# Attention kernel of a macaron layer: scores of two groups behind every second gate, one bank for both FFNs' sums, and other places for the projections and for the probabilities' low part

## The chip, the cores and the metric

The kernel runs on one core of one Trainium2 chip. The metric is the device time of the whole program in microseconds (us); less is better.

## The reference

One layer of the "macaron" form on x of 8 x 512 tokens with D = 512. LN is a layer norm without gains.

```
x = x + 0.5 * FFN(LN(x))        # FFN "A"
x = x + ATTN(LN(x))
x = x + 0.5 * FFN(LN(x))        # FFN "C", the same weights
FFN(x):  gu = x @ ternary(w_gate_up).T ; gate, up = split(gu)      # 2048 wide each
         h = silu(gate) * up ; return rms_norm(h) @ ternary(w_proj).T
ATTN(x): q, k, v = x @ Wq.T, x @ Wk.T, x @ Wv.T                     # 32 heads of 16
         scores = q @ k.T / 4, masked to a window of the 128 keys before each query
         return (softmax(scores) @ v) @ Wo.T
```

A query sees its own block of 128 tokens and the block ahead of it. In the first block of each sequence of 512 tokens there is only its own. The weights of the FFN are quantised to three values by groups of 64; the kernel does that on the chip too.

## The kernel before, in words

The 4096 tokens are 32 blocks of 128 rows (`NB` = 32). An instruction stream is written by hand for each engine, and semaphores order them; no scheduler moves anything. After the weights are prepared (the first 150 us or so), every engine runs the same loop `for step in range(FIRST_STEP, STEPS)` with a `step_of(step)` of its own. A block enters every 8 steps, and the stages of a block stand at fixed offsets: stage X of block b is at step 8b + X. What one step of an engine does, and in what order, is the order of the lines in its `step_of`. Below, r is the step modulo 8; **r = 1, 3, 5, 7 are called odd steps**.

- *FFN.* The hidden 2048 columns are 4 quarters of 512 (`NC` = 4). In the steady state A has its quarters at r = 0 to 3, C at r = 4 to 7, so each step has one quarter. TensorE (PE) multiplies its gate half (`up(.., 0, ps_g)`, 8 matmuls of 512 columns) and its up half (`up(.., 1, ps_u)`, 8 more), and two steps later the down product of it (`down`, 8 more, into `ps_y`). ScalarE (ACT) takes tanh of the gate, VectorE (DVE) multiplies (`gated`, L859; `hidden`, L865), ACT and DVE split the result in a high and a low f16 half (`hh`, L605 and L850), and a DMA transpose makes `ht` of it. `spread` gives the quarters of a few blocks at either end of the program other steps, so that there are steps without a quarter.
- *Attention.* The heads are 8 groups of 4. Group g of block b has its step at 8b + `SCORES` + g, one in every step. PE multiplies the scores (`scores`: 4 matmuls with only 48 rows of the array each, of 256 columns, the two halves of the array in turn), DVE adds the mask and takes the row maxima (`masked_max`, L876: 4 instructions, each with a read of its maximum), ACT takes bias and exps (L726, L731) and the high f16 half of the probabilities (L743), DVE the low half (L850, prob), two DMA transposes make `pt`, and PE multiplies by v (`prob_v`, 16 matmuls of 33 columns). After each second group DVE normalises (`normalise_o`, L886 to L891).
- *Projections.* Q, K, V and the output projection are 12 matmuls of 512 columns each (`project`) into one bank, `ps_m`. Q, K, V and the output projection stand at r = 0, 1, 3 and 7, at the end of PE's step.
- *PSUM.* There are eight banks: `ps_s` (two, scores), `ps_g`, `ps_u`, `ps_y` (two: one for A's sums and one for C's), `ps_o` and `ps_m`.

The order within a step of the steady state on PE is: gate, down (of two steps ago), up, scores of the next step's group, probabilities times v, a projection. PE waits in this order for `d_gate` and `d_h` (DVE has emptied `ps_g`, `ps_u`), `t_h` (ht has landed), `d_mx` (DVE has read the scores of the group before) and `t_ph`, `t_pl` (pt has landed).

On DVE a step is: `normalise_o`, `masked_max` of one group, the low part of q, k or v, `gated`, the low part of the last step's probabilities, `add_output`, `hidden`, the low part of the attention output (`oh`), `add_ffn`, the statistics of a layer norm (`norm_stats`, L841 to L845), the low part of `hh`. All DMAs of the loop are issued by SyncE (SP), in its order.

Of the kernel before, what the change touches and what calls it, by code (L numbers as in the profile page):

```python
# [15 lines left out]
P = 128  # L16
# [8 lines left out]
def macaron(nc, x, Wq, Wk, Wv, Wo, w_gate_up, w_proj, out):  # L25
# [55 lines left out]
    with ExitStack() as ctx:  # L81
# [174 lines left out]
        t_q, t_k, t_o = sem("t_q"), sem("t_k"), sem("t_o")  # L256
# [41 lines left out]
        assert len(AT_STEP) == len(GATES) == 2 * NB * NC - NC  # L298

# [99 lines left out]
        def _(sp):  # L399
# [55 lines left out]
            for step in range(FIRST_STEP, STEPS + 1):  # L455
# [7 lines left out]
                if b is not None:  # L463
                    sp.wait_ge(a_k, b + 1)
                    sp.wait_ge(d_k, b + 1)
                    need(sp, p_s, 16 * (b - 2))
                    transpose(kt[:, :, b % BPS, :], k4[:, :, :, :].rearrange("p a b c -> p (a b c)"), t_k)
                b, g = group_at(step, PROB)
                if b is not None:
                    need(sp, p_pv, 8 * b + g - 1)  # L470
                    sp.wait_ge(a_ph, 8 * b + g + 1)
                    first = first_half(b)
                    transpose(pt[:, g % 2, 0, first:2, :, :].rearrange("p a b c -> p (a b) c"),
                              prob[:, g % 2, 0, first:2, :, :].rearrange("p a b c -> p (a b c)"), t_ph[g % 2])
                    sp.wait_ge(d_pl, 8 * b + g + 1)
                    transpose(pt[:, g % 2, 1, first:2, :, :].rearrange("p a b c -> p (a b) c"),
                              prob[:, g % 2, 1, first:2, :, :].rearrange("p a b c -> p (a b c)"), t_pl[g % 2])
# [11 lines left out]
                if b is not None and in_steps("A", b):  # L489
                    normalised_t("A", b, p_up["A"], 8 * b)  # L490
                b = block_at(step, SPLIT_O)
# [7 lines left out]
                b = complete("C", step, 3)  # L499
# [3 lines left out]
                b = block_at(step, LN_A - 8)  # L503
# [98 lines left out]
        def _(act):  # L602
# [69 lines left out]
            def step_of(step):  # L672
# [13 lines left out]
                if b is not None:  # L686
                    need(act, t_k, 16 * b)
# [21 lines left out]
                if block_at(step, SPLIT_O) == LAST:  # L709
                    output_hi(LAST)  # L710
# [6 lines left out]

                b = block_at(step, SPLIT_O)
                if b is not None and b < LAST:
                    output_hi(b)  # L720
# [14 lines left out]
                s, bf, c = ffn_at(step)  # L735
                if s:
                    hidden_hi(s, bf, c, place(step), 4 * bf + c + 1 + (NC if s == "A" else 0))

                b, g = group_at(step, SCORES)
                if b is not None:  # L740
                    act.wait_ge(a_exp, 8 * b + g + 1)
                    need(act, t_ph[g % 2], 16 * (4 * b + g // 2))
                    act.activation(prob_part(prob[:, g % 2, 0, :, :, :], b), prob_f32(b, g), ACT.Copy).then_inc(a_ph, 1)  # L743

# [4 lines left out]
        def _(dve):  # L749
# [118 lines left out]
            def masked_max(b, g):  # L868
# [3 lines left out]
                for o in range(2):  # L872
                    dve.wait_ge(p_s, 16 * b + 2 * g + o + 1)
                    for pair in range(2):
                        hd = 4 * g + 2 * pair + o
                        m = dve.tensor_tensor_reduce(masked[:, g % 2, 2 * pair + o, first:2 * P],  # L876
                                                     ps_s[:, o * CH + pair * 2 * P + first:o * CH + (pair + 1) * 2 * P],
# [17 lines left out]
            def add_ffn(s, b, done):  # L895
                dve.wait_ge(p_dn[s], 4 * b + 4)
                dve.wait_ge(g_rms[s], b + 1)
                dve.scalar_tensor_tensor(out=slot(b), in0=ps_y[s][:, :], scalar=rms_inv[s][:, 0:1], in1=slot(b),  # L898
# [47 lines left out]
            def step_of(step):  # L946
                b, g = group_at(step, NORM)
                if b is not None and g % 2:
                    normalise_o(b, g // 2)

                b, g = group_at(step, SCORES)
                if b is not None:
                    masked_max(b, g)
# [31 lines left out]
                if block_at(step, SPLIT_O) == LAST:  # L985
                    output_lo(LAST)
# [292 lines left out]
```

## Time and profile before

| | |
|---|---|
| median of 3 runs | 2029.98 us (2029.53 to 2031.16) |
| the profiled execution | 2030.56 us, span of its profile 2028.7 us |
| PE busy | 1919.7 us, 95% |
| DVE busy | 1541.2 us, 76% |
| ACT busy | 1493.1 us, 74% |
| DMA queue q1 | 75.9% of 16 engines' span |
| granted clock of PE, mean | 0.98 |

The span is that of the profiled execution, from the first to the last instruction; 1.9 us of that execution's time lie around it. A group's busy time counts each matmul until its modelled end, which overlaps the start of the next, so groups of PE add up to more than the span. How far PE is from its peak is better read from the starts of successive groups in the timeline. Full speed is 2.4 GHz, and the lower level is half of it.

### The profile page before, as it was taken

The page shows a single profiled execution, that of the slowest core. Times are in us where ns is not written, and L with a number is a line of the kernel's source. Part 1 is how long each engine was busy: PE and PEld are TensorE (multiplying, and loading weights), DVE is VectorE, ACT ScalarE, POOL GpSimd, SP SyncE. Part 2 cuts the span into 40 slices and gives each one's busy share as a digit, 9 for nine tenths or more (in the row PEclk, how much of TensorE's full clock was granted, in tenths as well). Part 3 has the DMA queues.
Part 4 walks back from the last instruction along what each step waited for, and adds up shares of the span by engine and source line. Part 5 has one row for each costly group of instructions (what it writes and reads, how often), then busy time and mean ns, then how long its engine had stood idle before and what let it go on. Part 6 is the DMA issues. An engine that isn't in the chain of part 4 may idle for free. (4 is left out here: it accounts for less than half of the span.)

```text
span 2028.7 us, 37471 instructions
## 1 busy us (share of the span) xinstructions
PE 1919.7 (95%) x12447; PEld 898.9 (44%) x12688; DVE 1541.2 (76%) x4079; ACT 1493.1 (74%) x2871; POOL 510.9 (25%) x559
## 2 busy tenths in 40 slices
PE   6678899999999999999999999999999999999887
PEld 3353344444444444444444444444444444444332
DVE  8966788777876888777777888777786788777673
ACT  6837777777776777777776777777776777768672
POOL 2012222232223222322222223222223232221100
PEclk8889999999999999999999999999999999999898
DMA  7336888788887878777896788878886788768772
GB/s 233 121 71 112 147 153 147 132 141 159 149 156 126 156 145 153 136 145 150 154 159 125 138 155 153 149 131 154 159 155 120 141 153 165 144 120 154 131 136 52
DMA packets 1031648, 287.81 MB, mean 142 GB/s; under 512 B 1016096, under 2 KB 1017120, under 8 KB 1030944
## 3 DMA queue, kind: packets, MB, share of 16 engines
q1 hardware_dynamic: 1031456, 285.41, 75.9%
q8 instruction: 101, 1.65, 0.3%
q14 instruction: 91, 0.75, 0.1%
HBM read 25.17 MB, written 8.39 MB: 17 GB/s over the span
## 5 line engine op out<-in xcount | busy, mean ns | idle before, releaser
L731 ACT ACTIVATE masked<-masked,exp_bias,exp_scale 128x256 f32<-128x256 f32 (+1 forms) x1024 | 503.8, 562 | 8.6
L1095 PE MATMUL ps_yy<-wp_t,ht 128*128 128x512 bf16 x1978 | 481.0, 383 | 14.4 <-DMA ht<-hh 11.7
L1049 PE MATMUL ps_gu<-wgu_t,xt_A 128*128 128x512 bf16 x1940 | 473.8, 382 | 11.2 <-DVE hid L859 2.5
L1049 PE MATMUL ps_gu<-wgu_t,xt_C 128*128 128x512 bf16 x1958 | 472.6, 379 | 5.3 <-DMA xt_C<-xh 0.5
L605 ACT ACTIVATE hh<-hid 128x512 f16<-128x512 f32 x256 | 161.0, 629 | 276.3 <-DVE hid L865 271.0
L876 DVE CUSTOM_DVE_ANT_0 masked<-ps_s,mask 128x256 f32<-128x256 f32 (+1 forms) x1024 | 337.4, 385 | 0.7 <-PE ps_s L1085 0.6
L865 DVE SCALAR_TENSOR_TENSOR hid<-ps_gu,h_scale_u,hid 128x512 f32<-128x512 f32 x252 | 188.9, 750 | 185.0 <-PE ps_gu L1049 184.7
L1095 PEld LDWEIGHTS ps_yy<-wp_t,ht 128*128 128x128 f16 x2016 | 197.9, 99 | 254.5 <-DMA ht<-hh 13.5
L1049 PEld LDWEIGHTS ps_gu<-wgu_t,xt_A 128*128 128x128 f16 x2048 | 198.6, 98 | 243.3 <-issue 6.3
L1049 PEld LDWEIGHTS ps_gu<-wgu_t,xt_C 128*128 128x128 f16 x2048 | 193.4, 98 | 222.5 <-issue 2.4
L850 DVE TENSOR_TENSOR prob<-masked,prob 128x1024 f16<-128x1024 f32 (+1 forms) x256 | 278.9, 1089 | 2.4 <-ACT prob L743 2.4
L859 DVE SCALAR_TENSOR_TENSOR hid<-hid,ps_gu 128x512 f32<-128x512 f32 x256 | 175.8, 687 | 109.3 <-ACT hid L609 108.7
L544 POOL TENSOR_TENSOR xh<-xhat,xh 128x512 f16<-128x512 f32 x94 | 110.2, 1173 | 550.9 <-ACT xh L605 550.9
L850 DVE TENSOR_TENSOR hh<-hid,hh 128x512 f16<-128x512 f32 x256 | 176.2, 689 | 94.1 <-ACT hh L605 91.4
L743 ACT ACTIVATE prob<-masked 128x1024 f16<-128x1024 f32 (+1 forms) x256 | 239.2, 934 | 0.5
L609 ACT ACTIVATE hid<-ps_gu 128x512 f32<-128x512 f32 x256 | 150.1, 586 | 108.1 <-PE ps_gu L1049 104.4
L666 ACT ACTIVATE squares<-hid 128x512 bf16<-128x512 f32 x256 | 156.9, 613 | 0.0
L1107 PE MATMUL ps_om<-v,pt 128*128 128x33 f16 x3584 | 132.2, 178 | 5.8 <-DMA pt<-prob 5.8
L1107 PEld LDWEIGHTS ps_om<-v,pt 128*128 128x128 f16 x3584 | 106.7, 96 | 54.4 <-issue 47.2
L726 ACT ACTIVATE exp_bias<-row_max,prob_bias,neg_exp_scale 128x4 f32<-128x4 f32 x256 | 97.9, 382 | 30.1 <-DVE row_max L876 26.7
L1085 PE MATMUL ps_s<-kt,qt 48*128 48x256 f16 (+1 forms) x1024 | 93.7, 261 | 14.8 <-DVE row_max L876 14.8
L535 POOL TENSOR_TENSOR rstd_B<-var_eps_B,neg_half 128x1 f32<-128x1 f32 x32 | 28.5, 892 | 280.6 <-DVE var_eps_B L845 280.6
(148 smaller groups left out, 1892.8 us busy)
## 6 DMA issues: line engine op xcount, KB each, us to landing
stream<-in_L_attn_x_dram SPq DMA_DIRECT2D x32, 256.0 KB, 3.3
pt<-prob SPq DMA_TRANSPOSE x512, 3.2
out_dram<-stream SPq DMA_DIRECT2D x32, 256.0 KB, 2.4
prob<-in_L_ffn_w_gate_up_dram SPq DMA_DIRECT2D x4, 1024.0 KB, 5.6
ht<-hh SPq DMA_TRANSPOSE x256, 3.3
stream<-in_L_ffn_w_gate_up_dram SPq DMA_DIRECT2D x3, 1024.0 KB, 5.6
stream<-in_L_ffn_w_proj_dram SPq DMA_DIRECT2D x2, 1024.0 KB, 4.9
prob<-in_L_ffn_w_proj_dram SPq DMA_DIRECT2D x2, 1024.0 KB, 4.8
```

The lines of the kernel that those rows point to most:

```text
L605: act.activation(dst, src, ACT.Copy, scale=scale).then_inc(done, 1)
L609: act.activation(hid[:, n % 2, :], ps_g[:, :], ACT.Tanh, scale=0.5 * 2.0 ** -XS_LOG2).then_inc(a_tanh[s], 1)
L666: act.activation(squares[:, n % 2, :], hid[:, n % 2, :], ACT.Square, accum_out=sq_quarter[s][:, c:c + 1]).then_inc(a_sq[s], 1)
L731: t = act.activation(p, p, ACT.Exp, bias=exp_bias[:, 4 * g + h:4 * g + h + 1], scale=exp_scale[:, 0:1])
L743: act.activation(prob_part(prob[:, g % 2, 0, :, :, :], b), prob_f32(b, g), ACT.Copy).then_inc(a_ph, 1)
L850: dve.tensor_tensor(out=dst, in0=src, in1=hi, op=ALU.subtract).then_inc(done, 1)
L859: dve.scalar_tensor_tensor(out=hid[:, n % 2, :], in0=hid[:, n % 2, :], scalar=1.0, in1=ps_g[:, :], op0=ALU.add, op1=ALU.mult).then_inc(d_g ...
L865: dve.scalar_tensor_tensor(out=dst, in0=ps_u[:, :], scalar=scale, in1=hid[:, n % 2, :], op0=ALU.mult, op1=ALU.mult).then_inc(d_h[s], 1)
L876: m = dve.tensor_tensor_reduce(masked[:, g % 2, 2 * pair + o, first:2 * P], ps_s[:, o * CH + pair * 2 * P + first:o * CH + (pair + 1) * 2 ...
L1049: t = pe.matmul(bank[:, :], xt[s][:, part, k, :], wgu_t[:, k, at:at + CH], start=(k == 0 and part == 0), stop=(k == KD - 1 and part == 1))
L1095: t = pe.matmul(ps_y[s][:, :], ht[:, n % HRING, i, :], wp_t[:, 4 * c + i % 4, :], start=(c == 0 and i == 0), stop=(c == NC - 1 and i == 2 ...
L1107: t = pe.matmul(ps_o[:, at:at + VW], pt[:, g % 2, part, half, 2 * pair + o, :], v[:, at_block - 1 + half, hd, 0:VW], start=(n == 0), stop= ...
```

## The change

- The two sums `ps_y` of A and C become one bank. The bank freed is `ps_x`. A new table `ps_sc` gives even groups' scores the two banks of `ps_s`, and odd groups' scores the banks `ps_x` and `ps_m`; `ps_m` is the bank of the projections too.
- PE multiplies the scores of groups g and g+1 together, in every second step (g even, so r = 4, 6, 0, 2), behind the gate of the same step. The products with v stand between down and up. `scores` waits that the projection of two steps ago has been taken from `ps_m`, and each projection waits until DVE has read the scores of both groups (`d_mx`). The first down product of an FFN waits until the sum of the FFN before has been taken.
- The projections stand at r = 0 (Q), 2 (K), 4 (V) and 6 (output; the last block's stays where it was).
- DVE does `masked_max` of both groups in the even step, and the low part of the probabilities in the step of their exps, behind `hidden`. `normalise_o` and `add_ffn` stand ahead of `hidden`. The normalisation is one step earlier, and so are the split of the attention output (`SPLIT_O`) and C's layer norm.
- ACT makes the probabilities' high part ahead of the hidden split, not behind it.
- SP transposes the probabilities in the step of their exps. The transpose of k is two DMAs, of 4 and of 12 tiles, each with a semaphore of its own.

```diff
-    Q_AT, K_AT, V_AT = 8, 9, 11
+    Q_AT, K_AT, V_AT = 8, 10, 12
     SCORES = 12
-    PROB = SCORES + 1
     PV = SCORES + 2
-    NORM = PV + 1
-    SPLIT_O, WO_AT = NORM + 7, 23
-    LN_C, XHAT_C, SPLIT_C = 24, 25, 26
+    NORM = PV
+    SPLIT_O, WO_AT = NORM + 7, 22
+    LN_C, XHAT_C, SPLIT_C = 23, 24, 26
...
-    LAST_WO = 8 * LAST + WO_AT
+    LAST_WO = 8 * LAST + WO_AT + 1
...
-        ps_y = {"A": ps_yy[:, 0:CH], "C": ps_yy[:, CH:2 * CH]}
+        ps_y, ps_x = ps_yy[:, 0:CH], ps_yy[:, CH:2 * CH]
...
+        ps_sc = ((ps_s[:, 0:CH], ps_s[:, CH:2 * CH]), (ps_x, ps_m))
...
@@ vector, step_of @@
+                b, g = group_at(step, SCORES)
+                if b is not None and g % 2 == 0:
+                    masked_max(b, g)
+                    masked_max(b, g + 1)
...
+                b, g = group_at(step, SCORES)
+                if b is not None:
+                    prob_lo(b, g)
...
@@ tensor @@
+            def projections_taken(step):
+
+                for offset, done in ((Q_AT, d_q), (K_AT, d_k), (V_AT, d_v), (WO_AT, d_x2)):
+                    b = block_at(step, offset)
+                    if b is not None:
+                        pe.wait_ge(done, b + 1)
...
+                b, g = group_at(step, SCORES)
+                if b is not None and g % 2 == 0:
...
+                    need(pe, d_mx, 2 * (8 * b + g))
+                    projections_taken(step - 2)
...
+                    scores(b, g, ps_sc[0])
+                    scores(b, g + 1, ps_sc[1])
...
                 s, b, c = ffn_at(step - 2)
                 if s:
                     if c == 0:
-                        need(pe, d_x1 if s == "A" else d_x3, b)
+                        _, s0, b0, _ = QUARTERS[place(step - 2) - 1]
+                        pe.wait_ge(d_x1 if s0 == "A" else d_x3, b0 + 1)
                     down(s, b, c, place(step - 2))
...
                     pe.wait_ge(t_x["B"], 16 * (b + 1))
                     need(pe, d_x2, b - 1)
                     need(pe, d_v, b)
+                    need(pe, d_mx, 2 * groups_by(step + 1, SCORES))
```

The same wait on `d_mx` stands ahead of K, V and the output projection.

Two steps of PE (r = 5, 6) of a block in the steady state, before. L1049 is a gate or an up half, L1095 down, L1085 scores, L1107 probabilities times v, L1074 a projection:

```order
L1049 MATMUL ps_gu<-wgu_t,xt_C 128x512 x8
L1095 MATMUL ps_yy<-wp_t,ht 128x512 x8
L1049 MATMUL ps_gu<-wgu_t,xt_C 128x512 x8
L1085 MATMUL ps_s<-kt,qt 128x256 x4
L1107 MATMUL ps_om<-v,pt 128x33 x16
L1049 MATMUL ps_gu<-wgu_t,xt_C 128x512 x8
L1095 MATMUL ps_yy<-wp_t,ht 128x512 x8
L1049 MATMUL ps_gu<-wgu_t,xt_C 128x512 x8
L1085 MATMUL ps_s<-kt,qt 128x256 x4
L1107 MATMUL ps_om<-v,pt 128x33 x16
```

The same place in the change, from the down product of r = 5 to the output projection of r = 6 (an up half and a gate stand together in the third row):

```order
L1099 MATMUL ps_yy<-wp_t,ht 128x512 x8
L1111 MATMUL ps_om<-v,pt 128x33 x16
L1054 MATMUL ps_gu<-wgu_t,xt_C 128x512 x16
L1089 MATMUL ps_s<-kt,qt 128x256 x4
L1089 MATMUL ps_yy<-kt,qt 128x256
L1089 MATMUL ps_om<-kt,qt 128x256
L1089 MATMUL ps_yy<-kt,qt 128x256
L1089 MATMUL ps_om<-kt,qt 128x256
L1099 MATMUL ps_yy<-wp_t,ht 128x512 x8
L1111 MATMUL ps_om<-v,pt 128x33 x16
L1054 MATMUL ps_gu<-wgu_t,xt_C 128x512 x8
L1079 MATMUL ps_om<-wo,ot 128x512 x12
```

The eight score matmuls stand together in the even step, four of them into `ps_s` and four into `ps_yy` and `ps_om`, and the projection in `ps_om` follows 40 matmuls later in the same step.

DVE at the end of an odd step (r = 5) and the start of the next, in the change. L870 is `hidden`, L855 the low parts, L881 `masked_max`:

```order
L891 TENSOR_REDUCE o_sum<-ps_om 128x128
L892 RECIPROCAL row_inv<-ps_om 128x8
L896 TENSOR_TENSOR o_norm<-o_sum,row_inv 128x128
L903 SCALAR_TENSOR_TENSOR stream<-ps_yy,rms_inv_A,stream 128x512
L870 SCALAR_TENSOR_TENSOR hid<-ps_gu,h_scale_u,hid 128x512
L855 TENSOR_TENSOR prob<-masked,prob 128x1024
L855 TENSOR_TENSOR oh<-o_norm,oh 128x512
L846 BN_STATS st_B<-stream 128x6
L848 BN_AGGR mean_var_B<-st_B 128x2
L850 TENSOR_SCALAR var_eps_B<-mean_var_B 128x1
L855 TENSOR_TENSOR hh<-hid,hh 128x512
L881 ISA masked,row_max<-ps_s,mask 128x256
```

Before, the low part of `oh` and the statistics of B stood in different steps, and `prob` stood ahead of `hidden`; here all of them stand between `hidden` and the first of eight L881.

## Rows read from the trace of the kernel before

**Rows 1.** Busy time by stretch: us, busy (x count) of PE, PEld, DVE, ACT, POOL; PEclk; DMA share
```profile
186.90:246.30 59.40, 49.56 (x337) 22.08 (x340) 44.74 (x132) 45.44 (x87) 17.01 (x15) 0.94 0.84 140
400.00:800.00 400.00, 397.25 (x2616) 183.29 (x2667) 313.21 (x855) 306.86 (x603) 109.14 (x117) 1.00 0.83 148
1866.20:1962.30 96.10, 78.50 (x567) 34.84 (x577) 72.12 (x209) 72.39 (x134) 15.45 (x18) 0.89 0.73 134
```

**Rows 2.** Timeline of PE, steady state, one step and the next one's start: start, us, group
```profile
1025.43 1.89 PE L1049 MATMUL ps_gu<-wgu_t,xt_A 128*128 128x512 bf16 x8
1027.16 1.89 PE L1095 MATMUL ps_yy<-wp_t,ht 128*128 128x512 bf16 x7
1028.88 1.89 PE L1049 MATMUL ps_gu<-wgu_t,xt_A 128*128 128x512 bf16 x8
1030.71 0.39 PE L1085 MATMUL ps_s<-kt,qt 48*128 48x256 f16 x4
1031.03 0.57 PE L1107 MATMUL ps_om<-v,pt 128*128 128x33 f16 x16
1031.45 2.75 PE L1074 MATMUL ps_om<-wq,xt_B 128*128 128x512 f16 x12
1034.03 1.89 PE L1049 MATMUL ps_gu<-wgu_t,xt_A 128*128 128x512 bf16 x7
```

**Rows 3.** Timeline of DVE in the same steps: start, us, instruction [idle before <-releaser]
```profile
1028.59 1.22 DVE L850 TENSOR_TENSOR prob<-masked,prob 128x1024 f16<-128x1024 f32 x1
1029.73 0.74 DVE L982 SCALAR_TENSOR_TENSOR stream<-ps_om,out_scale,stream 128x512 f32<-128x512 f32 x1
1030.91 0.75 DVE L865 SCALAR_TENSOR_TENSOR hid<-ps_gu,h_scale_u,hid 128x512 f32<-128x512 f32 x1 [0.44 <-PE ps_gu L1049]
1031.58 0.69 DVE L841 BATCH_NORM_STATS2 st_C<-stream 128x6 f32<-128x512 f32 x1
...
1032.59 0.68 DVE L850 TENSOR_TENSOR hh<-hid,hh 128x512 f16<-128x512 f32 x1
1033.18 0.42 DVE L876 CUSTOM_DVE_ANT_0 masked<-ps_s,mask 128x256 f32<-128x256 f32 x1
...
1034.56 0.08 DVE L876 DVE_READ_ACCUMULATOR2_ANT row_max<- 128x1 f32 x1
...
1041.64 0.42 DVE L886 TENSOR_REDUCE o_sum<-ps_om 128x128 f32<-128x256 f32 x1
...
1042.47 0.42 DVE L876 CUSTOM_DVE_ANT_0 masked<-ps_s,mask 128x256 f32<-128x256 f32 x1
```

**Rows 4.** Timeline of ACT in the same steps
```profile
1027.36 0.60 ACT L609 ACTIVATE hid<-ps_gu 128x512 f32<-128x512 f32 x1 [1.24 <-PE ps_gu L1049]
...
1028.26 2.08 ACT L731 ACTIVATE masked<-masked,exp_bias,exp_scale 128x256 f32<-128x256 f32 x4
...
1032.91 1.04 ACT L743 ACTIVATE prob<-masked 128x1024 f16<-128x1024 f32 x1
```

**Rows 5.** The page's groups: splits of 512 columns on ACT (count, busy us, mean ns)
```profile
L605 ACT ACTIVATE hh<-hid 128x512 f16<-128x512 f32 x256 | 161.0, 629 | 276.3 <-DVE hid L865 271.0
```

**Rows 6.** DMA issues of the page: count, KB, us from issue to landing
```profile
pt<-prob SPq DMA_TRANSPOSE x512, 3.2
...
ot<-oh SPq DMA_TRANSPOSE x32, 3.3
```

**Rows 7.** Groups by form: the masks of the blocks that begin a sequence
```profile
L876 DVE CUSTOM_DVE_ANT_0 masked<-ps_s,mask 128x128 f32<-128x128 f32 x256 | 58.7, 285 | 0.6 <-PE ps_s L1085 0.6
```

**Rows 8.** Timeline of PE near the end of the program
```profile
1955.79 0.39 PE L1085 MATMUL ps_s<-kt,qt 48*128 48x256 f16 x4 [1.64 <-DVE row_max L876]
...
1956.80 3.19 PE L1095 MATMUL ps_yy<-wp_t,ht 128*128 128x512 bf16 x8
1961.37 0.55 PE L1107 MATMUL ps_om<-v,pt 128*128 128x33 f16 x16 [1.38 <-DMA pt<-prob]
...
1963.98 1.89 PE L1095 MATMUL ps_yy<-wp_t,ht 128*128 128x512 bf16 x8
...
1980.25 4.45 PE L1074 MATMUL ps_om<-wo,ot 128*128 128x512 f16 x12 [3.22 <-DMA ot<-oh]
```

More of the change, by code:

```diff
@@ L298, in macaron @@
         assert len(AT_STEP) == len(GATES) == 2 * NB * NC - NC
+        assert all(QUARTERS[n][1:3] == QUARTERS[n - n % NC][1:3] for n in range(len(QUARTERS)))
         def gate_at(step):
@@ L453, in _ @@
                 load_x(b)
-            for step in range(FIRST_STEP, STEPS + 1):
+            for step in range(FIRST_STEP, STEPS + 2):
                 b = block_at(step, Q_AT + 1)
@@ L466, in _ @@
                     need(sp, p_s, 16 * (b - 2))
[L467 to L477, printed above, removed]
+                    for part, pairs in enumerate((slice(0, 4), slice(4, HEADS // 2))):
+                        transpose(kt[:, pairs, b % BPS, :],
+                                  k4[:, 2 * pairs.start:2 * pairs.stop, :, :].rearrange("p a b c -> p (a b c)"),
+                                  t_k[part])
                 b = block_at(step, SPLIT_B)
@@ L498, in _ @@
                     hidden_t(s, b, c, place(step))
-                b = complete("C", step, 3)
+                b = complete("C", step, 4)
                 if b is not None:
@@ L946, in step_of, with add_output, prob_lo @@
             def step_of(step):
[L947 to L953, printed above, removed]
+                def add_output(b):
+                    dve.wait_ge(p_wo, b + 1)
+                    dve.scalar_tensor_tensor(out=slot(b), in0=ps_m[:, :], scalar=out_scale[:, 0:1], in1=slot(b),
+                                             op0=ALU.mult, op1=ALU.add).then_inc(d_x2, 1)
+                def prob_lo(b, g):
+                    need(dve, t_pl[g % 2], 16 * (4 * b + g // 2))
+                    take_lo(prob_part(prob[:, g % 2, 1, :, :, :], b), prob_f32(b, g),
+                            prob_part(prob[:, g % 2, 0, :, :, :], b), a_ph, 8 * b + g + 1, d_pl)
                 b = block_at(step, Q_AT + 1)
@@ L993, in step_of @@
                         attention_weight(n)
-                b = block_at(step, WO_AT + 1)
-                if b is not None and b < LAST:
-                    add_output(b)
+                b = complete("A", step, 2)
+                if b is not None:
+                    add_ffn("A", b, d_x1)
+                b = complete("C", step, 2)
+                if b is not None:
+                    add_ffn("C", b, d_x3)
                 s, bf, c = ffn_at(step)
@@ L1069, in attention_weight, with project, scores @@
                 t.then_inc(a_tr, 1)
-            def project(m, tokens, done):
+            def project(m, tokens, done, bank):
                 for k in range(KD):
                     for n, (part, w) in enumerate(((0, wat_hi), (0, wat_lo), (1, wat_hi))):
-                        t = pe.matmul(ps_m[:, :], tokens[:, part, k, :], w[m][:, k, :], start=(k == 0 and n == 0),
+                        t = pe.matmul(bank[:, :], tokens[:, part, k, :], w[m][:, k, :], start=(k == 0 and n == 0),
                                       stop=(k == KD - 1 and n == 2))
                 t.then_inc(done, 1)
-            def scores(b, g):
+            def scores(b, g, banks):
                 at_block = b % BPS
@@ L1246, in step_of @@
                     pe.wait_ge(d_q, b + 1)
-                    project(K, xt["B"], p_k)
+                    need(pe, d_mx, 2 * groups_by(step + 1, SCORES))
+                    project(K, xt["B"], p_k, ps_m)
                 b = block_at(step, V_AT)
```

121 lines of the change are left out of this document (59 added, 62 removed).

## The prediction

> **What bounds the kernel now.** First the busy time by stretch [rows 1]. In the steady state PE is busy for 397.25 of 400 us at full clock, while DVE is busy for 78% of the time and ACT for 77%. Only there does PE's own work set the time; it lasts from step 28 (about 246 us) to step 252 (about 1866 us), 112 pairs of steps. In the ramp (186.9 to 246.3 us) PE is busy for 83%, and near the end (1866.2 to 1962.3 us, steps 252 to 267) for 82% at a mean clock of 0.89. There DVE and ACT hold PE up, each 75% busy itself.
>
> A busy PE isn't a PE at its peak, so the timeline of PE comes next [rows 2]. Read the starts. The gate takes 1.73 us (1025.43 to 1027.16), down 1.72, up with what follows it 1.83, scores 0.32, the products with v 0.42, a projection 2.58. Gate, down and up have eight matmuls of one size each, so 0.10 of up's 1.83 us is a pause ahead of the scores. A step is 6.02 us, and a pair of steps with its one projection 14.62.
>
> Then DVE and ACT in the same steps [rows 3, 4], for how long after PE they can start and how long a thing keeps its engine (again from start to start): `hidden` starts 0.30 us after up is done (1030.61) and keeps DVE for 0.67; a low part of the probabilities 1.14; statistics 1.01 (1031.58 to 1032.59); a low part of 512 columns 0.59; normalising 0.83; four masks 1.38, with 0.08 for the last read. The tanh starts 0.20 after the gate is done, the exps 0.90 after the tanh's start, and exps and high part take 2.08 and 1.04.
>
> **What the change takes from PE.** Of two groups of scores, one pause of 0.10 goes. The second four matmuls stand behind four of their own kind. Eight full-size matmuls take 1.72 us, so 256 columns take 0.108. The two halves of the array have separate matmuls; if they run side by side, four cost 0.21 and not 0.32, as the other 0.11 is the change back to the whole array. I take this, since 0.32 is less than the 0.43 that four cost one after the other. The gain is 0.21 a pair; its bounds are 0.10 (the pause alone) and 0.30. A pair becomes 14.41: even step 1.73 + 0.10 + 0.32 + 0.21 + 1.72 + 0.42 + 1.73 + 2.58 = 8.81, odd step 1.73 + 1.72 + 0.42 + 1.73 = 5.60. Over 112 pairs that is **-23.5 us** (-11 to -34). The Trainium skill ("TensorEngine Tiling (Array Packing)", "Key Properties") says that changing the tiling mode drains the array, which is what the 0.10 looks like; by that rule the pause goes with every change of mode, whatever stands around it, and the term stays as it is.
>
> **What it adds: projections wait for masks.** An odd group's scores lie in `ps_m`, so the projection that ends the even step waits for eight masks, which DVE starts only when its odd step is over. Let T be the time at which PE ends the odd step. PE reaches the projection at T + 8.81 - 2.58 = T + 6.23.
>
> - r = 7 to 0, ahead of Q. ACT: tanh at T - 5.60 + 1.73 + 0.20, exps 0.90 later, high part done at T + 0.4, in time. DVE: `hidden` T + 0.30 to 0.97, low part of the probabilities to 2.11, statistics of C to 3.12, low part of `hh` to 3.71, then eight masks, 2.76 + 0.08: T + 6.55. With 0.05 for the semaphore (an estimate) PE starts at 6.60: **0.37 us late**.
> - r = 5 to 6, ahead of the output projection. `normalise_o` can start 0.3 us after the products with v, at T - 5.60 + 3.87 + 0.30 = T - 1.43, and is done at T - 0.55. Now ACT splits the attention output first (0.63 [rows 5]) and makes the high part of the probabilities after it: done at T + 1.15. DVE: low part of the probabilities 1.19 to 2.33, of `oh` to 2.93, statistics of B to 3.94, `hh` to 4.53, masks to 7.37; PE at 7.42: **1.19 us late**. The transpose of `oh`, issued at about T + 3.7 behind two of the probabilities, lands 3.3 us later [rows 6], at about 7.0. It is the next to be late, and covers half of what an earlier mask would give.
> - r = 1 to 2 and 3 to 4, ahead of K and V: no statistics in the odd step. `hh` ends at T + 2.70, the masks at 5.54, and PE comes 0.64 after them. No wait.
> - Blocks that begin a sequence (every fourth) have masks of 128 columns, 285 ns each where the others have about 420 [rows 7, 3], and half of the probabilities. 8 x 0.135 + 0.5 is more than 1.19: no wait.
>
> The other new waits cost nothing in the steady state. The one bank of sums is free when `add_ffn` is done, at about T + 0.1 (behind `normalise_o`), and down comes at T + 2.36. The projection is taken from `ps_m` by T - 2.9, and the scores come at T + 1.83. The first 4 tiles of kt are issued at about T - 2.3 and needed at T + 1.83; the other 12 only two steps later. The k transpose as two DMAs is one more of 31 a block. SP waits for the low part at r = 5 with `oh` and `hh` queued behind it, and `hh` isn't needed before T + 10.5.
>
> 21 of the blocks in the steady state aren't the first of a sequence: 21 x (0.37 + 1.19) = **+32.8 us**. Each of these waits rests on a chain of ten durations and I allow 0.2 on either: 24 to 41 us.
>
> **The ends.** In steps 252 to 267 many steps have no quarter, so PE reaches the projection sooner and waits for the masks longer. Laid out by hand from the same durations, the pairs from 252 on take 12.0, 15.8, 15.0, 10.3, 12.0, 16.5, 10.8 and 8.6 us, 101 in all, against the 96.1 of before [rows 1]. In three of them PE stands for 4 to 5 us and its projection runs at half clock, as 1980.25 shows (4.45 us for twelve matmuls instead of 2.75 [rows 8]). At the last output projection the 3.22 us wait for `ot` should go, since the products with v and the normalisation come earlier, and with it the 1.7 us of half clock. Together **+3 us**, and the bounds are -8 and +12, since a hand layout of unsteady steps can be off by half a microsecond in each. The ramp has four such pairs (steps 20 to 27): **+1.5 us** (-3 to +5).
>
> **Sum.** -23.5 + 32.8 + 3 + 1.5 = +13.8 on the profiled execution's 2030.56 gives 2044.4. The median of the runs is 0.6 lower: **2044 us**, 0.7% slower.
>
> **The rivals.**
>
> *Faster: masks come in time* (24%). If the masks end about 0.4 us sooner, Q no longer waits, the output projection waits for 0.8 at most, and the balance tips. The point is 0.9 us of waiting a block (21 x 0.9 = 19 us). For it: in the two pairs the sum hangs on some tenths of a chain of ten, and near the end PE is held up by `row_max` of the very group before [rows 8], a wait that pairs do away with. Against it: DVE has no idle time left in my chain for r = 5 and 7. With 0.4 us a block: -23.5 + 8 = -15 and nothing from the ends, 2015 us; with 0.8, 2023.
>
> *No change* (13%): waits of 1.0 to 1.3 a block and the ends even, 2026 to 2034.
>
> *The clock falls* (8%, one of the slower cases). A pause of 1.64 us near the end is followed by matmuls at half speed (3.19 us for eight instead of 1.89), one of 1.38 isn't [rows 8]. My wait for the output projection is 1.2 us, of which some 1.0 would show as idle. Should it tip the clock to 1.2 GHz, each costs 1.7 more: 21 x 1.7 = 36, 2080 us. The Trainium skill ("TensorE: Matmul & The Clock Gate", "HAM oscillation") describes a kernel whose every tile starts cold after a pause for data; by that rule it would be 2080. No row here shows it for pauses as short as mine.
>
> *The scores don't get cheaper* in pairs is in the range: 0.10 a pair instead of 0.21 adds 12 us, 2056.
>
> **Chances.** About 0.2% (4 us) can be told from no change. Forecast and its slower neighbours 55%, clock 8%: slower 0.63; faster 0.24; same 0.13. The range: 2044 with its own bounds (waits +-8, scores -10 to +12, ends -14 to +12, not all at once) is 2028 to 2062. Toward the faster rival it goes down to 2020, which leaves out about half of that; the clock's case is left out above.
>
> **What would show it.** In the changed kernel's PE waits, the projections wq and wo should wait for `row_max` about 0.2 to 0.4 and 1.0 to 1.2 us, 21 times each, and wk and wv not. The scores' first start in an even step should be 1.83 after the gate's, down 0.53 after that. The steady state should have blocks of 57.6 us where no mask waits and 59.2 us elsewhere, against 58.5. Wrong would be: no wait at wo (the faster rival), wait on `ot` instead, projections of 4.4 us in the middle of the program (the clock), or down starting 0.64 us after the scores.

## The result, and the profile after

| | before | after |
|---|---|---|
| median of 4 runs | 2029.76 us (2027.77 to 2031.16) | 2074.77 us (2073.75 to 2121.51) |
| ratio, 95% interval | | 1.0221 (1.0201 to 1.0241) |
| profiled execution, span | 2030.56, 2028.7 us | 2074.78, 2072.9 us |
| up to the gate of step 28 | 246.3 us | 255.1 us |
| steps 28 to 252 | 1620.1 us | 1645.0 us |
| step 252 to the start of the last output projection | 113.9 us | 125.9 us |
| from there to the end | 48.45 us | 46.85 us |

The change is slower by 2.2%, where 0.7% was forecast; the time lies outside the range. The highest run of after was a disturbed one and counts in no ratio. The sign was right, the size wrong in all three stretches: of the 44.2 us, the steady part takes 24.9 (forecast 9.3), the start 8.8 (1.5), and all that follows step 252 takes 10.5 (3).

The busy time of after, the page's first line and three stretches (columns as in [rows 1]: PE, PEld, DVE, ACT, POOL, then PE's clock):

```profile
PE 1919.5 (93%) x12688; PEld 913.7 (44%) x12688; DVE 1548.3 (75%) x4079; ACT 1507.5 (73%) x2871; POOL 481.0 (23%) x559
```

```profile
186.90:255.10 68.20, 54.47 (x366) 24.66 (x365) 47.49 (x142) 48.62 (x93) 16.93 (x15) 0.90 0.71 130
400.00:800.00 400.00, 389.64 (x2611) 183.47 (x2609) 306.67 (x840) 304.18 (x594) 100.29 (x116) 1.00 0.81 145
1900.10:2008.30 108.20, 81.79 (x594) 37.73 (x593) 72.86 (x209) 72.86 (x136) 16.03 (x18) 0.87 0.69 124
```

PE has as much to do as before (1919.5 us of busy time against 1919.7); DVE and ACT show 7 and 14 us more, and both are idle for a quarter of the span. PE's busy time in 400 us of the steady part fell from 397.25 to 389.64 [rows 1], at full clock: it waits.

**What PE gained.** The timeline of PE in after, the end of an odd step and the even step with the output projection:

```profile
1033.25 3.61 PE L1054 MATMUL ps_gu<-wgu_t,xt_C 128*128 128x512 bf16 x16
1036.80 0.39 PE L1089 MATMUL ps_s<-kt,qt 48*128 48x256 f16 x4
1037.03 0.27 PE L1089 MATMUL ps_yy<-kt,qt 48*128 48x256 f16 x1
...
1037.34 1.90 PE L1099 MATMUL ps_yy<-wp_t,ht 128*128 128x512 bf16 x8
1039.08 0.56 PE L1111 MATMUL ps_om<-v,pt 128*128 128x33 f16 x16
1039.48 1.89 PE L1054 MATMUL ps_gu<-wgu_t,xt_C 128*128 128x512 bf16 x8
1042.47 2.75 PE L1079 MATMUL ps_om<-wo,ot 128*128 128x512 f16 x12 [1.10 <-DVE row_max L881]
1045.06 1.89 PE L1054 MATMUL ps_gu<-wgu_t,xt_C 128*128 128x512 bf16 x8
```

Down starts 0.54 us after the scores; 0.53 was forecast. The second group costs 0.21 us, and the gain of 0.21 a pair is there. (Between the scores and the projection stand 8, 16 and 8 matmuls, 32 and not the 40 that the section on the change gives.) Read the last wait against the starts: up starts at 1039.48 and takes 1.73, so PE could have gone on at 1041.21, and it started at 1042.47. It lost 1.26 us and the row shows 1.10. Each shown wait of such a kind is 0.16 us too small, because the end of the matmul before it is modelled.

**What it lost in the steady part.** PE's waits in after from 270 to 1870 us (columns: us in all, times, longest):

```profile
PE ps_om L1079 <- DVE row_max L881: 21.4, 34, 1.1
PE ps_om L1079 <- DMA ot<-oh: 19.0, 14, 1.9
PE ps_s L1089 <- DMA kt<-k: 0.5, 1, 0.5
```

That is 40.9 us shown in 49 waits, and with 0.16 for each 48.7. One more wait of Q, at 1877.55, lies behind this window and before step 252, which makes 49.2 (the kernel before has one wait in its whole steady part, 0.3 us shown). Less the 23.5 of the scores this is 25.7, and the steady part is 24.9 longer: the account closes within 1 us. By places: Q waits in 21 steps, 0.29 or 0.30 us shown, always for the masks. The output projection waits in **all 28** blocks: in 14 for the masks (1.10 each), in 14 for the transpose `ot`, and seven of those 14 are the blocks that begin a sequence. Here are three more such rows, of a Q, a block that begins a sequence and one that doesn't:

```profile
1057.33 2.75 PE L1079 MATMUL ps_om<-wq,xt_B 128*128 128x512 f16 x12 [0.30 <-DVE row_max L881]
1100.62 2.76 PE L1079 MATMUL ps_om<-wo,ot 128*128 128x512 f16 x12 [0.56 <-DMA ot<-oh]
1393.25 2.76 PE L1079 MATMUL ps_om<-wo,ot 128*128 128x512 f16 x12 [1.75 <-DMA ot<-oh]
```

The same even step on DVE, ahead of the wait at 1042.47:

```profile
1035.29 0.75 DVE L870 SCALAR_TENSOR_TENSOR hid<-ps_gu,h_scale_u,hid 128x512 f32<-128x512 f32 x1 [0.26 <-PE ps_gu L1054]
1036.14 1.22 DVE L855 TENSOR_TENSOR prob<-masked,prob 128x1024 f16<-128x1024 f32 x1
1037.28 0.68 DVE L855 TENSOR_TENSOR oh<-o_norm,oh 128x512 f16<-128x512 f32 x1
1037.88 0.69 DVE L846 BATCH_NORM_STATS2 st_B<-stream 128x6 f32<-128x512 f32 x1
...
1038.89 0.68 DVE L855 TENSOR_TENSOR hh<-hid,hh 128x512 f16<-128x512 f32 x1
1039.49 0.42 DVE L881 CUSTOM_DVE_ANT_0 masked<-ps_s,mask 128x256 f32<-128x256 f32 x1
...
1042.24 0.68 DVE L864 SCALAR_TENSOR_TENSOR hid<-hid,ps_gu 128x512 f32<-128x512 f32 x1
```

The scores are done at 1037.34, but DVE has only just begun the low part of `oh`; the statistics and the low part of `hh` come next, and it starts on the masks at 1039.49. The two that read `ps_m` are the last of eight. And SP's queue at that place, and at the late one of 1393.25 (SPq is the time that issuing takes):

```profile
1036.11 2.62 SPq L408 DMA_TRANSPOSE pt<-prob  x2
1038.82 1.29 SPq L408 DMA_TRANSPOSE ot<-oh  x1
...
1386.24 2.80 SPq L408 DMA_TRANSPOSE pt<-prob  x2
1389.13 2.10 SPq L408 DMA_TRANSPOSE ot<-oh  x1
```

`oh` is complete at 1037.96, but SP is busy with the two transposes of the probabilities until 1038.73, and only then issues `ot`. It landed at 1042.10, 3.28 us later and before the masks were done (1042.32). In the 14 blocks that wait for the masks `ot` lands 3.05 to 3.38 us after its issue. In the seven others inside a sequence, as at 1393.25, it takes 3.79 to 4.38 us. In four of those the issue itself was long (1.42 to 2.15 us), in three it was the usual 1.29; what makes them slow is open.

**What it lost near the end.** PE's waits from step 252 to the last output projection, in after (1900 to 2026 us):

```profile
PE ps_om L1079 <- DVE row_max L881: 11.1, 5, 4.6
PE ps_yy L1099 <- DMA ht<-hh: 10.1, 3, 5.1
PE ps_om L1079 <- DMA ot<-oh: 5.5, 1, 5.5
PE ps_s L1089 <- DMA kt<-k: 2.2, 1, 2.2
```

Before, the same stretch had 10.1 us of waits for `row_max` ahead of the scores, and 7.0 us of all others. Behind three of the pauses of after the projection runs at about half speed (before had one such in this stretch, Q's at 1895.16, and the one that ends it, at 1980.25):

```profile
1919.75 4.44 PE L1079 MATMUL ps_om<-wo,ot 128*128 128x512 f16 x12 [4.56 <-DVE row_max L881]
...
1934.56 5.28 PE L1079 MATMUL ps_om<-wq,xt_B 128*128 128x512 f16 x12 [3.76 <-DVE row_max L881]
...
1975.49 5.30 PE L1079 MATMUL ps_om<-wo,ot 128*128 128x512 f16 x12 [5.54 <-DMA ot<-oh]
```

Twelve matmuls take 4.4 to 5.3 us there instead of 2.75. The start of the program has three more of this kind, the longest behind 6.00 us for `ot` at 218.57.

### The profile page after: what moved, and what is told of

It reads as the page before. It is cut to its first block and busy times, and to the rows that moved or that the text cites. A ratio compares the mean times of both kernels' runs of the same rounds, so it can differ in the third digit from the quotient of the medians.

```text
span 2072.9 us, 37964 instructions
## 1 busy us (share of the span) xinstructions
PE 1919.5 (93%) x12688; PEld 913.7 (44%) x12688; DVE 1548.3 (75%) x4079; ACT 1507.5 (73%) x2871; POOL 481.0 (23%) x559
## 5 line engine op out<-in xcount | busy, mean ns | idle before, releaser
L1054 PE MATMUL ps_gu<-wgu_t,xt_A 128*128 128x512 bf16 x2048 | 485.3, 383 | 4.2 <-DVE hid L864 2.7
L1054 PE MATMUL ps_gu<-wgu_t,xt_C 128*128 128x512 bf16 x2048 | 477.7, 379 | 0.0
L855 DVE TENSOR_TENSOR prob<-masked,prob 128x1024 f16<-128x1024 f32 (+1 forms) x256 | 278.4, 1087 | 95.2 <-ACT prob L744 92.1
L1099 PEld LDWEIGHTS ps_yy<-wp_t,ht 128*128 128x128 f16 x2016 | 188.5, 98 | 255.4 <-issue 26.5
L870 DVE SCALAR_TENSOR_TENSOR hid<-ps_gu,h_scale_u,hid 128x512 f32<-128x512 f32 x252 | 189.2, 751 | 138.3 <-PE ps_gu L1054 126.9
L1054 PEld LDWEIGHTS ps_gu<-wgu_t,xt_A 128*128 128x128 f16 x2048 | 192.5, 98 | 224.3 <-issue 10.8
L855 DVE TENSOR_TENSOR hh<-hid,hh 128x512 f16<-128x512 f32 x256 | 175.2, 685 | 13.1 <-ACT hh L611 13.1
L881 DVE CUSTOM_DVE_ANT_0 masked<-ps_s,mask 128x256 f32<-128x256 f32 (+1 forms) x512 | 168.6, 385 | 1.2 <-PE ps_om L1089 0.7
L1111 PEld LDWEIGHTS ps_om<-v,pt 128*128 128x128 f16 x3584 | 126.5, 96 | 63.8 <-issue 6.6
L1079 PE MATMUL ps_om<-wo,ot 128*128 128x512 f16 x384 | 94.9, 400 | 50.6 <-DMA ot<-oh 30.6
L891 DVE TENSOR_REDUCE o_sum<-ps_om 128x128 f32<-128x256 f32 x128 | 54.3, 424 | 93.0 <-PE ps_om L1111 92.9
```

The costliest lines, as they stand in the source:

```text
L855: dve.tensor_tensor(out=dst, in0=src, in1=hi, op=ALU.subtract).then_inc(done, 1)
L870: dve.scalar_tensor_tensor(out=dst, in0=ps_u[:, :], scalar=scale, in1=hid[:, n % 2, :], op0=ALU.mult, op1=ALU.mult).then_inc(d_h[s], 1)
L1054: t = pe.matmul(bank[:, :], xt[s][:, part, k, :], wgu_t[:, k, at:at + CH], start=(k == 0 and part == 0), stop=(k == KD - 1 and part == 1))
L1099: t = pe.matmul(ps_y[:, :], ht[:, n % HRING, i, :], wp_t[:, 4 * c + i % 4, :], start=(c == 0 and i == 0), stop=(c == NC - 1 and i == 2 * N ...
L1111: t = pe.matmul(ps_o[:, at:at + VW], pt[:, g % 2, part, half, 2 * pair + o, :], v[:, at_block - 1 + half, hd, 0:VW], start=(n == 0), stop= ...
```

## The experiments

**Theory 1:** the projections wait because DVE comes late to the eight masks. **Theory 2:** behind the masks stands a second, separate wait, for `ot`, late in SP's queue, and the two cover each other. All times are medians. Each ratio is against runs of the kernel before from the same session (medians of 2028.2, 2028.2 and 2029.6 us for experiments one to four, five to eight, and nine and ten), so it isn't quite the quotient of the column. The stretches are those of the first table, in us, from the one profiled execution of each kernel.

| kernel | us | ratio (95%) | to step 28 | 28 to 252 | 252 to last output projection |
|---|---|---|---|---|---|
| before | 2029.76 | 1 | 246.3 | 1620.1 | 113.9 |
| after | 2074.77 | 1.0221 (1.0201 to 1.0241) | 255.1 | 1645.0 | 125.9 |
| masks of ps_m first | 2062.73 | 1.0164 (1.0145 to 1.0182) | 248.0 | 1640.1 | 124.7 |
| ot early | 2052.99 | 1.0118 (1.0102 to 1.0133) | 251.8 | 1630.5 | 123.5 |
| both | 2026.81 | 0.9994 (0.9985 to 1.0004) | 243.5 | 1612.8 | 120.4 |
| statistics behind masks | 2053.33 | 1.0122 (1.0107 to 1.0137) | 250.3 | 1631.7 | 122.7 |
| first + SP's order alone | 2034.13, one run | | 247.3 | 1615.9 | 122.3 |
| first + DVE's order alone | 2069.25, one run | | 253.0 | 1643.7 | 125.2 |
| both, ends reordered | 2043.44 | 1.0077 (1.0061 to 1.0092) | 252.1 | 1613.0 | 133.6 |
| the same + statistics | 2037.76 | 1.0051 (1.0037 to 1.0064) | 248.8 | 1606.1 | 131.7 |
| both + statistics | 2020.03 | 0.9953 (0.9940 to 0.9966) | 243.5 | 1607.8 | 117.5 |
| the same, ot first | 2010.43 | 0.9911 (0.9896 to 0.9926) | 244.3 | 1601.1 | 117.6 |

### One: the masks of ps_m first

```diff
-                    masked_max(b, g)
-                    masked_max(b, g + 1)
+                    masked_max(b, g + 1, (1,))
+                    masked_max(b, g, (0, 1))
+                    masked_max(b, g + 1, (0,))
...
-                need(pe, d_mx, 2 * groups_by(step + 1, SCORES))
+                need(pe, d_mm, groups_by(step + 1, SCORES) // 2)
```

Here (1,) is the half whose two masks read `ps_m`, and `d_mm` counts that half alone.

> One part alone: of the eight masks the two that read the bank shared with the projections (ps_m) are done first, and the projections wait for these two only. Theory 1 (the projections wait for DVE, which comes late to its eight masks): the 34 waits for row_max in the steady part (21.4 us shown, 27 us with 0.17 us that each hides) vanish, 2048 us. Theory 2 (behind the masks stands a second wait, for ot's transpose, which SP issues after the two transposes of the probabilities): Q's waits vanish (21 x 0.47 = 10 us), but at the output projection the wait for the masks (1.10 us shown) turns into one for ot of 0.6 to 1.1 us in all blocks, so 2060 us (2056 to 2064). The exps of the even group begin 0.7 us later in either case, with ACT idle for 3.1 us ahead of them, at no cost.

2062.73 us. The waits in the steady part (270 to 1850 us):

```profile
PE ps_om L1085 <- DMA ot<-oh: 32.4, 27, 2.1
PE ps_s L1095 <- DMA kt<-k: 1.3, 3, 0.8
```

No wait for `row_max` is left, and the output projection waits for `ot` in every block, 1.2 us each. Theory 1 alone falls (it wanted 2048); the second wait is there, as theory 2 says. Most of the 12 us that this edit saves comes from the start (7.1); the steady part gave 4.9. Two of the waits are of interest for the clock, since only one of them was followed by half speed:

```profile
563.41 4.39 PE L1085 MATMUL ps_om<-wo,ot 128*128 128x512 f16 x12 [2.10 <-DMA ot<-oh]
...
974.96 2.76 PE L1085 MATMUL ps_om<-wo,ot 128*128 128x512 f16 x12 [2.02 <-DMA ot<-oh]
```

### Two: ot early

```diff
                     sp.wait_ge(a_ph, 8 * b + g + 1)
...
+                    output_t(step)
                     sp.wait_ge(d_pl, 8 * b + g + 1)
...
-                    prob_lo(b, g)
                     take_lo(oh[:, 1, :], o_norm[:, :], oh[:, 0, :], a_oh, b + 1, d_ol)
+                    prob_lo(b, g)
```

> The other part alone: o's low part goes ahead of the probabilities' low part on DVE, and SP transposes oh between the two transposes of the probabilities, 1.3 us earlier. Theory 2: the 14 waits for ot in the steady part (19.0 us shown, 21.4 in all) vanish; in the 7 of them that are in blocks inside a sequence the wait for the masks of 1.27 us shows in their place, so 12 us less: 2062 us (2057 to 2066), with 1.10 us at the output projection and 0.30 us at Q in 21 blocks each. Theory 1, if ot's waits were only a by-product of SP's slow issues at those places: no change, 2075 us.

2052.99 us, 9 less than expected. The steady part (270 to 1850 us) went as expected, with 40 waits for the masks of 24.1 us in all:

```profile
PE ps_om L1084 <- DVE row_max L886: 24.1, 40, 0.9
PE ps_om L1084 <- DMA ot<-oh: 2.1, 3, 1.0
```

It is 14.6 us shorter than in after (12 expected), and the two ends are 5.8 shorter, which I had not counted.

### Three: both

> Both edits together. Theory 2 (two separate waits that cover each other): nearly all of the steady part's 48.8 us goes, which neither edit alone gives (their savings of 15 and 12 us add to 27), and steps 28 to 252 take 1600 us (1645.0 now): 2030 us in all, down to 2022 if the start's waits for row_max (10.4 us) shrink too. Rival, that a third stage (the matmul of the next gate waiting for gated values or hidden, or the transposes of the probabilities now 1.3 us late for P V) takes up what is freed: 2045 to 2060 us, with new waits on DVE's hidden or on pt.

2026.81 us; nothing can be told from the kernel before. One and two alone save 12.0 and 21.8 us, 33.8 together; both at once save **48.0**. In the steady part it is 4.9 and 14.6 alone, and 32.2 together. What they save together beyond their sum is what the two waits had covered for each other. The steady waits left:

```profile
PE ps_yy L1110 <- DMA ht<-hh: 4.7, 7, 1.0
PE ps_om L1090 <- DMA ot<-oh: 4.5, 9, 0.9
PE ps_s L1100 <- DMA kt<-k: 0.7, 2, 0.5
```

A third stage does show, `ht`, though not one that the rival named, and it takes 4.7 us, not 15 or more. The steady part was expected at 1600 and took 1612.8: these waits, 9.9 us shown and 2.9 that 18 rows hide, are the difference. The total came out near the expected 2030 because the ends gave what the steady part did not. The start is now 243.5 us, less than before the change: its 8.8 us were these two waits. The stretch behind step 252 keeps 6.5 us more than before.

### Four: the statistics behind the masks

```diff
-                b = block_at(step, LN_B)
+                b = block_at(step, LN_B + 1)
...
-                b = block_at(step, LN_C)
+                b = block_at(step, LN_C + 1)
```

Both stand behind `masked_max` now, in the even step.

> The masks' place is kept, but the statistics of norms B and C (1.01 us of DVE each) move behind the masks of the next even step. Theory 1: the masks end 1.0 us sooner wherever they were waited for: Q's wait (0.30 us shown, 0.47 in all) goes, the output projection's falls from 1.27 to 0.26 us: 31 us less, 2044 us. Theory 2: Q's goes (10 us), the output projection stays behind ot's landing at 0.9 to 1.1 us: 2061 us (2056 to 2065).

2053.33 us. Another way to earlier masks, with the same floor below it (270 to 1850 us):

```profile
PE ps_om L1079 <- DMA ot<-oh: 28.4, 28, 2.0
```

The time lies between the two theories' numbers, below theory 2's range. The mechanism is theory 2's: all waits for masks go, and 28 waits for `ot` of 1.0 us remain. The steady part gave 13.3 us; the other 8 came from the ends.

### Five and six: which half of "ot early" it is

Both start from the first experiment, whose only wait at the output projection is `ot`. One takes SP's half of the second edit, the other DVE's.

> The kernel with the masks of ps_m first, and of the edit on ot only SP's half: SP transposes oh between the probabilities' two parts, DVE keeps its order (probabilities' low part, then o's). Theory 2a (ot is late because it stands behind a transpose on SP): SP can issue it when o's low part ends, 0.9 us sooner, so the 27 waits for ot in the steady part (32.4 us shown with the masks of ps_m first alone) fall to about 27 x 0.3 = 8 us: 2036 to 2042 us. Theory 2b (it is late because DVE writes o's low part second): they stay near 25 to 30 us and the time near 2058 us.

> The kernel with the masks of ps_m first, and of the edit on ot only DVE's half: o's low part ahead of the probabilities' low part, while SP keeps its order. Theory 2a: SP waits 0.6 us longer for the probabilities' low part and issues ot behind it 0.5 us later than before, so the waits for ot grow from 32.4 us shown to about 27 x 1.7 = 46 us: 2070 to 2078 us. Theory 2b: they fall by 0.6 us each, to 16 us: 2045 us.

Each was executed once, so differences of a few us are not told apart. SP's order alone: 2034.13 us, the steady waits for `ot` fall from 32.4 to 4.9 us. DVE's order alone: 2069.25 us, and they rise to 35.3. The rows of the two, in this order (270 to 1840 us):

```profile
PE ps_om L1090 <- DMA ot<-oh: 4.9, 9, 1.2
```

```profile
PE ps_om L1085 <- DMA ot<-oh: 35.3, 27, 2.3
```

The place in SP's queue decides. That DVE writes o's low part second isn't the cause; with it first and SP unchanged, SP waits longer for the probabilities' low part, and `ot` behind it is later still. I had expected 46 us of waits there, so the delay was smaller than my 0.5 us. Once SP's order is changed, DVE's may add a little: both edits together took 2026.81 us, 7.3 less than this one execution, 3.1 of it in the steady part.

### Seven and eight: the ends reordered

Theory 3: at the ends `ht` is late because it stands behind the probabilities' parts on ACT, DVE and SP. In steps below 28 and from 252 on it goes first on all three:

```diff
+                if s and at_end(step):
+                    hidden_hi(s, bf, c, place(step), 4 * bf + c + 1 + (NC if s == "A" else 0))
+
                 b, g = group_at(step, SCORES)
                 if b is not None:
                     act.wait_ge(a_exp, 8 * b + g + 1)
```

and likewise `hh`'s low part ahead of `prob_lo`, and `hidden_t` ahead of the transposes of the probabilities.

> Both edits (masks of ps_m first, ot early), and in the steps before 28 and from 252 on the FFN's hidden parts go ahead of the probabilities' on ACT, DVE and SP. Theory 3 (what the change lost at the ends beyond the steady waits is ht, which stands behind the probabilities' parts on three queues and has no filler there): the 8 waits for ht after 1856 us (19.4 us shown with both edits) fall by a third to a half, steps 252 to the last output projection take 112 to 116 us in place of 120.35, and the time is 2019 us (2015 to 2023), below the kernel before. Rival: with so little work left, each matmul waits for its predecessors' chain whichever part goes first, and pt then waits instead: 2024 to 2030 us, with waits for pt of 5 us or more.

2043.44 us, 17 **slower** than with both edits (22 between the two profiled executions), and all of it in the start (+8.6 us) and near the end (+13.2). The output projections near the end show why, first with both edits, then with the ends reordered too:

```profile
1874.20 5.30 PE L1090 MATMUL ps_om<-wo,ot 128*128 128x512 f16 x12 [2.86 <-DMA ot<-oh]
...
1927.43 4.45 PE L1090 MATMUL ps_om<-wo,ot 128*128 128x512 f16 x12 [4.00 <-DMA ot<-oh]
```

```profile
1886.89 5.30 PE L1104 MATMUL ps_om<-wo,ot 128*128 128x512 f16 x12 [6.59 <-DMA ot<-oh]
...
1946.58 4.50 PE L1104 MATMUL ps_om<-wo,ot 128*128 128x512 f16 x12 [6.02 <-DMA ot<-oh]
```

The waits for `ht` from step 252 to the end did shrink, from 19.4 to 13.3 us, as theory 3 said. But those for `ot` grew from 6.9 to 14.2, and those for `kt`, `row_max` and `pt` from 4.9 to 13.3. So theory 3 falls as a way to save time: attention's chain from the masks to `ot` is shorter of time at the ends than `ht`, and the hidden parts ahead of it make the projections later.

> As the one before, and the statistics of norms B and C behind the masks of the next even step. In the steady part hidden's low part comes 1.0 us sooner in the steps with statistics, so the 7 waits for ht (4.7 us shown) vanish, those for ot (9, 4.5 us) stay: 6 us less than the kernel before it, 2013 us (2009 to 2018). Rival: the later statistics make the split of norm C late for its up projection, with waits for xt_C in place of those for ht: no gain or some loss, 2019 to 2025 us.

2037.76 us: 5.7 less than the one before it, where 6 were expected, and the 10 waits for `ht` in the steady part are gone. The absolute number was off with theory 3, on which it was built.

### Nine and ten: the two edits without the reordered ends

> Both edits (masks of ps_m first, ot between the probabilities' two transposes) and the statistics of norms B and C behind the masks, with the ends as the change has them. The steady part should take 1606 us as with the ends reordered (1606.09), the ends as with both edits alone (243.5 to step 28, 120.4 from step 252 to the last output projection, 46.7 behind it): 2017 us of span, 2019 us in all (2015 to 2022), below the kernel before. Rival: that the statistics behind the masks cost at the ends, where the reordered ends hid it: 2022 to 2027 us.

2020.03 us, as expected: the kernel with both edits and later statistics is faster than the kernel before by 0.5%.

The last one takes from the failed seventh what it taught, and moves `ot` ahead of both transposes of the probabilities:

```diff
+                b = block_at(step, SPLIT_O)
+                if b is not None:
+                    sp.wait_ge(d_ol, b + 1)
+                    need(sp, p_wo, b)
+                    transpose(ot[:, :, :, :].rearrange("p a b c -> p (a b) c"), flat(oh[:, :, :]), t_o)
                 b, g = group_at(step, SCORES)
                 if b is not None:
                     need(sp, p_pv, 8 * b + g - 1)
```

> The same with SP transposing oh ahead of both transposes of the probabilities. In the steady part SP could issue it 0.65 us sooner (when o's low part ends), so the last 8 waits for ot (5.6 us shown) go: 1600 us. At the end, where o's low part stood ready 1.6 us before SP came to it (1922.5 against 1924.13), each of the two waits for ot (2.9 and 4.0 us) shrinks by 1.3 to 1.6 us, and with luck the projection behind it keeps the full clock: 117 us from step 252 to the last output projection. Together 2010 us (2005 to 2015). Rival: the probabilities' transposes, 1.3 to 1.9 us later, are now waited for by P V (rows with pt, none in the steady part so far), and the time stays at 2019 us or goes up.

2010.43 us, ratio 0.9911 (0.9896 to 0.9926): **19 us faster than the kernel before**, and 64 faster than the change as it was made. Its steady waits (270 to 1840 us), and the stretch 400 to 800:

```profile
PE ps_om L1085 <- DMA ot<-oh: 1.2, 4, 0.4
PE ps_s L1095 <- DMA kt<-k: 0.9, 1, 0.9
```

```profile
400.00:800.00 400.00, 398.45 (x2691) 189.13 (x2689) 316.38 (x866) 312.25 (x607) 100.79 (x115) 1.00 0.85 149
```

The steady part is 1601.1 us, 19.0 under before. With the 2.1 us of waits and 0.8 that the rows hide added, that is 22 of the 23.5 us that the scores in pairs were to give. P V doesn't wait for the later `pt`. Near the end the two projections run at full speed, after pauses of 2.0 and 2.3 us:

```profile
1862.66 2.76 PE L1085 MATMUL ps_om<-wo,ot 128*128 128x512 f16 x12 [2.03 <-DMA ot<-oh]
...
1914.37 2.76 PE L1085 MATMUL ps_om<-wo,ot 128*128 128x512 f16 x12 [2.34 <-DMA ot<-oh]
```

That stretch did not get shorter all the same (117.6 against 117.5), since `ht` is waited for instead: 16.3 us in 8 waits, where the ninth kernel had 13.2 in 6.

## Why the prediction was wrong in size, point by point

**What the change takes from PE: right.** 0.54 us from the scores to down against 0.53 forecast, 1.83 from the gate to the scores as forecast. The last experiment, with hardly a wait left, shows 22 of the 23.5 us.

**The wait at Q: right.** 0.30 us shown, 0.46 in all, against 0.37, 21 times; none in blocks that begin a sequence, and none at K and V. Over 21 blocks the tenth makes 2 us.

**The wait at the output projection: the step that failed.** Its masks were right (1.26 against 1.19). The sentence that broke is "the transpose of `oh` [...] lands [...] at about 7.0. It is the next to be late", taken as cover only, and with it "blocks that begin a sequence: [...] no wait". PE comes at T + 6.23, so a landing at T + 7.0 is a wait of 0.8 wherever masks are short; my own number said so and I priced only the masks. (0.8 of 1.19 is also two thirds, not the "half" that the prediction says `ot` covers.) In the seven blocks that begin a sequence this costs 7.6 us shown, 8.8 in all: seven times 0.8 is 5.4, and the rest comes from landings up to 4.1 us after the issue where I had taken the median, 3.3. In seven others `ot` landed after the masks, 3.8 to 4.4 us after its issue: 1.8 us lost in each and not 1.19, another 4.2. With 2 us from Q, 1 from the masks' 0.07 and 0.7 from one wait for `kt` this is the 16 us by which the waits were off (+49.2 against +32.8). One sum of this part is off without effect: `normalise_o` is done at T - 0.60 (-1.43 + 0.83), not T - 0.55.

**The ends: mis-sized.** The last output projection was as forecast, without wait and at full clock: 46.85 us from it to the end, 1.6 less than before. But the eight pairs of steps that I laid out at 101 us took 108.2, and with the 1.6 gained behind them the end of the program costs 10.5 us in all, not 3. Read from the gates' starts in the timeline the pairs took 12.1, 15.6, 16.0, 10.4, 12.4, 18.1, 14.5 and 9.0 us. The first five were laid out within 1 us each; the sixth and seventh (16.5 and 10.8 in the layout) hold 5.3 of the 7.2 us that it missed. Their long waits are for `ot` (5.54 us at 1975.49) and for `ht` (5.10 at 1992.87), which the layout, following PE and the masks, did not treat as chains of their own. The sum had a slip besides: 101 against 96.1, less the 3.22 us wait and the 1.7 of half clock, is 0 and not +3. That wait did go, but 2.85 us for `ht` at 2013.00 took its place. The start was priced at +1.5 by the same layout and was +8.8. Both kernels begin step 20 at 186.9 us; from there to step 28 after shows 6.6 us of waits for `row_max`, 6.0 for `ot` and 1.1 of others, 13.7 in all, where before shows 9.6. The rest of the 8.8 is not split up; the third experiment shows that it goes with the two waits.

**The rivals.** *Faster: masks come in time* was wrong about this kernel and partly right about the mechanism; the first experiment brings the masks in time and is still slower than before, as `ot` takes their place. *The clock falls* was wrong for this kernel: in the whole steady part the clock stayed at 1.00 through 28 pauses of 0.56 to 1.87 us shown. It was close, though. Pauses for `ot` of 2.10 us (first experiment, at 563.41), 2.00 (fourth, at 1087.97) and 2.26 and 2.01 (DVE's order alone, at 568.36 and 686.80) stand in the same steady part and were followed by projections of 4.1 to 4.5 us, while others of 2.02 and 2.00 (at 974.96 and 982.00 of the first and the last of these kernels) were not. The Trainium skill ("TensorE: Matmul & The Clock Gate", "HAM oscillation") tells of a kernel whose every tile starts cold after waits for data of some 3 to 5 us. The ends here agree, where pauses of 3.8 to 6.0 us come before projections of 4.4 to 5.3 us. What the prediction called that rule's 2080 carried it over to waits of 1.2 us, and there the steady rows speak against it.

**Still open.** From step 252 to the last output projection even the best kernel takes 3.7 us more than before (117.6 against 113.9), with waits for `ht`; behind it, it takes 2.9 less. Why some transposes of `oh` land later than others is open too. Putting `ht` first made it worse. A plan of its own for these steps, with one group of scores per step as before, wasn't tried.

## What to carry to other kernels

When two things must arrive before an instruction, work out both times against the moment at which the engine could start, and price the later one in each kind of block; removing the first wait alone shows only the difference to the second. Where such a time holds a transfer, price its slow cases too and not only the median. Here each fix alone gave 12 and 22 us and both 48. Merging two small pieces of work to spare one engine 0.2 us makes their consumer work in bursts: before doing it, find out what is queued behind the burst on that consumer, let it begin with the piece whose buffer someone waits for, and put the transfer with the nearest deadline first in its DMA queue.

## What the runs showed of the hardware

- Issuing the same transpose from SP takes different times. These are SP's issues of `ot` (ns, min/median/max) in after, where nearly all come within 0.1 us of another transpose's issue, and in the last kernel, where SP has been idle for 1.5 us or more:

```profile
L408 SPq DMA_TRANSPOSE ot<-oh x32: 1232/1290/2153, 214.7 to 2022.8; - x32
```

```profile
L409 SPq DMA_TRANSPOSE ot<-oh x32: 1232/1232/1244, 207.8 to 1959.6; - x32
```

  A short pause does not secure the quick issue: with SP's order alone SP is idle for 0.65 us ahead of most of them, and five of the 32 still took 2.06 to 2.52 us. Nor does a quick issue secure a quick landing: in the last kernel `ot` landed 3.2 to 5.0 us after its issue.

- The length of the last pause alone does not tell whether PE's clock falls. In the last kernel a pause of 2.03 or 2.34 us left the twelve matmuls behind it at full speed (2.76 us), and in the first experiment 2.02 us did so where 2.10 did not. In after, early in the program, one of 1.66 us came before twelve at half speed; PE had waited 3.10 us for `pt` 9 us earlier, and the granted clock had been at the lower level from 168.9 to 175.7 us:

```profile
178.93 4.44 PE L1079 MATMUL ps_om<-wq,xt_B 128*128 128x512 f16 x12 [1.66 <-DVE row_max L881]
```

- An idle time that the trace shows for PE ahead of a matmul is 0.16 us less than what PE lost by the starts of its groups (1.10 shown, 1.26 lost), which over 49 waits is 8 us.
